# The causal stage's division of the probabilities by their row sum: from VectorE (three heads) and ScalarE (one) to GpSimd (all four)

## The reference, cut to what matters

```python
scores = einsum('bhqd,bhkd->bhqk', q, k) / sqrt(64)
scores = where(causal, scores, finfo.min)
attn = softmax(scores, axis=-1)      # exp(x - max), divided by the row's sum
out = einsum('bhqk,bhkd->bhqd', attn, v)
```

## Time and profile before

| what | us |
|---|---|
| time, median of 3 runs | 1265.08 (1264.76 to 1265.37) |
| the profiled execution: its time | 1265.95 |
| the profiled execution: its span | 1264.1 |
| causal stage, first to last score | about 516 to 958 |
| one round of the causal stage | 55.8 |

### The profile page before, as it was taken

How to read it: one execution, slowest core, us unless ns; L and a number is a source line. 1 busy time by engine, 2 the same in 40 slices (tenths; PEclk the granted TensorE clock), 3 DMA queues, 4 the chain that set the end, 5 groups by cost and what they waited for, 6 DMA issues and landing times.

```text
span 1264.1 us, 27532 instructions
## 1 busy us (share of the span) xinstructions
PE 1079.2 (85%) x7484; PEld 982.7 (78%) x7484; DVE 1011.4 (80%) x3184; ACT 777.1 (61%) x2299; POOL 327.9 (26%) x544
## 2 busy tenths in 40 slices
PE   4699999999999992899999999999997349989892
PEld 1478888878888882689999989999996338888892
DVE  5599998989899998688888888888886716665655
ACT  2266666666566663688787878777776315554541
POOL 4455554545545448000000101000000220000013
PEclk9599999999999997699999999999999559999997
DMA  8600000000000000000000000010000345554413
GB/s 308 205 23 2 23 22 1 21 1 21 8 15 21 1 1 22 22 1 23 2 21 0 21 0 21 5 66 0 1 1 12 105 151 149 148 158 138 134 44 102
DMA packets 37400, 63.78 MB, mean 50 GB/s; under 512 B 3419, under 2 KB 23707, under 8 KB 37147
## 3 DMA queue, kind: packets, MB, share of 16 engines
q1 hardware_dynamic: 28604, 51.69, 13.1%
q10 hardware_dynamic: 7168, 6.88, 1.7%
q0 software_dynamic: 1536, 4.20, 1.1%
HBM read 45.92 MB, written 16.84 MB: 50 GB/s over the span
## 4 chain that ended last, share of the span: by engine, by line
PE 64%; DVE 16%; issue 8%; ACT 6%; DMA 2%; POOL 1%; ACTq 1%; DVEq 1%; SPq 1%; POOLq 0%
PE psO L621 14%; PE psS L593 9%; PE psX L604 8%; PE psP L640 8%; PE psY L675 5%; PE psS L792 4%; PE psX L792 3%; PE psT L651 3%; DVE pbuf L1185 3%; PE psT L660 2%; PE psO L813 2%; PE psP L813 2%; DVE pbuf L1201 2%; DVE bufB L1207 2%; DVE bufA L1243 1%
## 5 line engine op out<-in xcount | busy, mean ns | idle before, releaser
L880 ACT ACTIVATE pbuf<-pbuf,nmax 128x256 f32<-128x256 f32 (+3 forms) x512 | 266.9, 522 | 172.9 <-DVE nmax L1185 162.3
L621 PE MATMUL psO<-bufB 128*128 128x256 f32 x1632 | 257.4, 294 | 11.9 <-DVE bufB L1211 11.2
L593 PE MATMUL psS<-bufA 128*128 128x256 f32 (+3 forms) x1024 | 216.5, 317 | 19.9 <-DVE bufA L1243 16.9
L621 PEld LDWEIGHTS psO<-bufB 128*128 128x128 f32 x1632 | 213.5, 190 | 23.1 <-issue 12.7
L1207 DVE TENSOR_TENSOR bufB<-psX,bufB 128x512 fp32r<-128x512 f32 x272 | 186.7, 686 | 29.0 <-ACT bufB L853 27.0
L853 ACT ACTIVATE bufB<-psX 128x512 fp32r<-128x512 f32 x272 | 160.4, 590 | 59.5 <-PE psO L621 48.8
L593 PEld LDWEIGHTS psS<-bufA 128*128 128x128 f32 x1024 | 149.4, 194 | 37.5 <-DVE nmax L1185 26.0
L604 PE MATMUL psX<-idn,pbuf 128*128 128x128 f32 x1088 | 167.2, 276 | 2.7 <-DVE bufB L1207 2.2
L640 PE MATMUL psP<-wbufs,hTh 128*128 (+1 forms) x512 | 163.0, 360 | 1.6 <-DVE bufB L1236 1.6
L1201 DVE TENSOR_SCALAR pbuf<-pbuf,rden 128x256 f32<-128x256 f32 (+3 forms) x384 | 154.3, 457 | 4.5
L604 PEld LDWEIGHTS psX<-idn,pbuf 128*128 128x128 f32 x1088 | 124.5, 141 | 18.0 <-issue 8.4
(11 more groups left out here) (196 smaller groups left out, 2304.0 us busy)
## 6 DMA issues: line engine op xcount, KB each, us to landing
mrawV<-in_w_moe SPq DMA_DIRECT2D x32, 384.0 KB, 3.2
mrawB<-in_w_moe SPq DMA_DIRECT2D x32, 384.0 KB, 3.3
xg<-uN SPq DMA_DIRECT2D x1, 5248.0 KB, 23.8
yg<-uN SPq DMA_DIRECT2D x1, 5248.0 KB, 37.9
xin<-xg ACTq DMA_DIRECT2D x10, 384.0 KB, 3.8
wraw<-in_w_attn SPq DMA_DIRECT2D x8, 384.0 KB, 3.2
wraw<-in_w_ffn SPq DMA_DIRECT2D x8, 384.0 KB, 3.0
yg<-modb ACTq DMA_DIRECT2D x9, 256.0 KB, 2.2
```

The lines of the kernel that those rows point to most:

```text
L593: last = mm(psS[j % 2][:, 0:n], qT[:, s % NT, j * P:(j + 1) * P], kT[:, c, k0:k0 + n], start=(c == 0), stop=(c == 1))
L621: last = mm(psO[:, 0:2 * P], lhsT, pairs(pT)[:, r], start=(k == 0 and n == 0), stop=(k == L.ntiles(s) - 1 and n == 5))
L880: nc.scalar.activation(pj, pj, ACT.Exp, bias=nmax[:, s % 4, j:j + 1], scale=-1.0, accum_out=sums[:, s % 4, j:j + 1]).then_inc(a_exp, 1)
```

## The change

In the causal stage GpSimd now multiplies all four heads by the reciprocal. It does so in its step s for the unit s-1, in front of that step's `split_piece`. VectorE keeps the reciprocal, VectorE and ScalarE lose their multiplications, and PE waits for one semaphore, `g_norm`, in place of two. The windowed stage stays as it was.

```diff
 def step(g, s, L=L):                      # GpSimd
     ...
+    if L is LB and exists(g, s - 1):
+        wait(pool, v_rden, L.unit(g, s - 1))
+        n = L.ntiles(s - 1) * P
+        for j in range(QM):
+            pj = probs[:, (s - 1) % 4, j, 0:n]
+            apart(pool)
+            last = nc.gpsimd.tensor_scalar(pj, pj, rden[:, (s - 1) % 4, j:j + 1], None, ALU.mult)
+        last.then_inc(g_norm, 1)
     if s in (0, 1, 2) and exists(g, NT):
         split_piece(g + 1, s)

 def turn_probs(g, s, k):                  # TensorE
-    if k == 0:
+    if k == 0 and L is LA:
         wait(pe, v_norm, L.unit(g, s))
         wait(pe, a_norm, L.unit(g, s))
+    elif k == 0:
+        wait(pe, g_norm, L.unit(g, s) - NT * NKV)

 def normalise(g, s):                      # ScalarE
     wait(act, v_rden, L.unit(g, s))
-    for j in range(L.by_vector, QM):
+    for j in range(L.by_vector, QM if L is LA else 0):
...
-    last.then_inc(a_norm, 1)
+    if L is LA:
+        last.then_inc(a_norm, 1)

 def normalise(g, s):                      # VectorE
...
+    if L is LB:
+        return
     for j in range(L.by_vector):
```

More of the change, by code:

```diff
@@ L334, in build @@
         a_norm = sem("a_norm")
+        g_norm = sem("g_norm")
         s_X = sem("s_X")
```

## The result

The changed kernel takes 1313.62 us in the median (1310.91 to 1315.83, 4 runs) against 1265.00 us before (1264.76 to 1265.37, 4 runs). The ratio is 1.0386 with an interval of 1.0362 to 1.0410: slower by 48.6 us. The forecast was 1312 us. The profiled execution took 1313.7 us with a span of 1311.9.

What follows compares the result with a forecast made beforehand. The prediction took TensorE, busy 96.5 of 100 us, to bound the causal stage. Its terms, 28.6 + 8.1 + 2.4 + 9.2 - 1.6 = +46.7 us on a median of 1265.08, gave 1312 us, range 1274 to 1345.

Steps and rivals of the forecast that it cites:

- Term 1: Rounds 1 to 6: tile 2's division queues behind a weight piece waiting for TensorE; six pauses of 4.8 us, +28.6 us.
- The price of a multiplication: On GpSimd, taken from its one-operation TENSOR_SCALAR: 1.53 us at length 512, 1.20 us at 384.
- rivals A and B: GpSimd multiplies at the CAST's price, 1276 us, chance 0.13; or nearer its two-operation price, about 1395 us, chance 0.1.
- Term 2: 512-long units elsewhere in the causal stage: GpSimd's division comes 0.9 us late for TensorE, nine times, +8.1 us.
- Term 3: End of the causal stage: GpSimd finishes the last division at 965.6, TensorE took these probabilities at 963.15, +2.4 us.
- Term 4: TensorE's clock falls behind four of the six long pauses, 2.3 us each: +9.2 us, bounds 0 and 13.8.
- The relief (-1.6): VectorE's saved multiplications shorten TensorE's 0.26 us pause for the key write by 0.1 us, 16 times: -1.6 us.
- The sum: 28.6 + 8.1 + 2.4 + 9.2 - 1.6 = +46.7 us, added to the median of 1265.08 us.

Runs made afterwards that it cites:

- three heads: Changed kernel with GpSimd dividing heads 0 to 2 and ScalarE head 3: ratio 1.0251; with the third weight piece also issued one step later, 0.9997.
- one instruction: Changed kernel with GpSimd dividing all four heads in one two-input multiplication, third weight piece left in step 2: 1291.54 us, ratio 1.0195.
- two heads: Changed kernel with GpSimd dividing heads 0 and 1 only, VectorE head 2, ScalarE head 3, third weight piece in step 2: 1289.86 us, ratio 1.0201.
- one head: Changed kernel with GpSimd dividing head 0 only, VectorE heads 1 and 2, ScalarE head 3, third weight piece in step 2: 1305.32 us, ratio 1.0273.
- single instruction: Changed kernel with one two-input multiplication for all four heads and the third weight piece issued in step 3: 1264.78 us, ratio 0.9972.
- piece 2 a step later: Changed kernel with GpSimd's third weight piece issued in step 3 instead of 2, behind the division of tile 2: 1283.93 us, ratio 1.0149.

## Why the prediction was right, point by point

**The blocked division (Term 1, +28.6).** Right and shown. Six pauses of 4.74 to 4.76 us, 28.5 in all, and one moved line removes them. The formula also holds over the dose. With the piece (2.10 us in the prediction, 2.05 in the expectations), the division, 0.15 for the wake-up and 2.13 off, it gives, forecast against measured: four heads 4.8 against 4.75; three heads 3.7 against 3.54; one instruction 2.8 against 2.57; two heads 2.5 against 2.32; one head 1.3 against 0.73. It is up to 0.25 us too long, and 0.6 us at one head, of which 0.35 is TensorE's own lateness there.

**The price of a multiplication.** 1.53 us forecast and 1.564 measured at 512, 1.20 and 1.242 at 384. The row to go by was the TENSOR_SCALAR of the same kind in the earlier trace rows, not the CAST, and rivals A and B fell with it. At 128 and 256 it is 605 and 924 ns, so the fixed part is nearer 0.29 than 0.2 us. The rule of the Trainium skill ("GPSIMD Engine Reference", section 4.1) that one-input work runs roughly at line rate does not hold for this instruction: the same 512 elements take 610 ns as a CAST and 1564 ns here.

**The 512-long units (Term 2, +8.1).** Nine pauses of 0.71 to 0.82 us, about 7.0 in all. That tile 3 of rounds 1 to 6 is forgiven was right: with the long pause gone, these six came back. With 5.4 us or less for the division the pause is gone altogether, as three heads and the single instruction showed.

**The stage's end (Term 3, +2.4).** The last pause is 2.52 us, and one of 1.32 us stands ahead of it. They took the place of pauses of 1.57 and 0.60 us for VectorE's `bufB`, so +1.7 net. Behind the last the clock fell for 3.4 us, about 3.4 x (1 - 1/1.8) = 1.5 us lost: 3.2 in all.

**The clock (Term 4, +9.2).** The term that was mis-sized, by its count. All six long pauses had a fall behind them, not four, and so had the last pause of the stage. Here are the stretches of the kernel before, of the changed one and of that with piece 2 a step later (columns as in the earlier trace rows):

```profile
529.23:977.24 448.01, 426.24 (x3207) 403.79 (x3207) 389.26 (x1286) 352.14 (x1046) 29.30 (x36) 1.00 0.03 11
524.16:1026.15 501.99, 443.66 (x3206) 418.42 (x3206) 343.90 (x1097) 327.28 (x983) 302.62 (x293) 0.96 0.04 11
526.67:990.47 463.80, 428.85 (x3207) 403.54 (x3207) 343.71 (x1097) 327.02 (x983) 302.67 (x293) 1.00 0.04 12
```

TensorE does the same matmuls in all three (one record is missing in the second). It is busy 17.4 us longer in the changed kernel, and 2.6 us longer with the piece moved, where it never works at half clock: some 0.15 us for each of 17 pauses. The other 14.8 us belong to seven falls, 2.1 us each, so the price of 2.3 us was near enough. I had taken from the earlier trace rows that a pause of 2.4 us leaves the clock at 1.00. The same pause of the windowed stage looks otherwise in the kernel without division:

```profile
477.75 0.98 PE L624 MATMUL psO<-bufB 128*128 128x256 f32 x6 [2.41 <-DVE bufB L1217]
```

```profile
480.00:482.00 2.00, 2.00 (x11) 2.00 (x11) 1.07 (x3) 0.98 (x2) 0.41 (x1) 0.50 0.02 4
```

With one head, and with one instruction not moved, it had a fall behind it too. In the causal stage pauses of 2.57 us had one six times in six and 2.32 us four times in six; of the two of 2.5 us at the stage's end (changed, and piece 2 later) one; those of 0.8 us none. So what follows a pause of 2.3 to 2.5 us differs with the same work around it, and one row of one execution was too little to build on.

**The relief (-1.6).** Measured -1.9 without any division. The size was right by luck. It was to come from the pauses of 0.26 us, which stayed as they were; it came from the first round and the stage's end. I had also named `add_y` as the start of the round trip; moving it left the pauses as they were, and the trip starts with the scores of head 2 behind it. The conclusion, that the pause of 0.62 us starts with TensorE and so can't be relieved, holds with that correction.

**The sum.** By the three rows, TensorE's idle time in the stretch grew from 21.8 to 58.3 us, +36.6, where pauses and relief were put at 28.6 + 8.1 + 2.4 - 1.6 = 37.5. Its busy time grew by 17.4, where the clock was put at 9.2. Against the median the forecast of +46.7 met +48.6, and that closeness is partly luck: a sum 7.3 us short against the stretch was offset by an earlier rise of the clock ahead of it, as far as the two profiled executions show.

**What stays open:** why equal pauses of 2.32 us had a fall behind them at four places and not at two, and whether fetched instructions are what stalled VectorE at the loop's start with one head.

## What to carry to other kernels

An engine that is 10% busy is not free at every moment: before giving it work with a due time, look at what stands ahead of that work in its queue and what that waits for, since here one weight copy that waited for TensorE turned a hidden division into six pauses of 4.8 us. A pause of the bounding engine can have a second price in its clock; here it was about 2.1 us behind four of six pauses of 2.32 us and behind all the longer ones in the middle of the stage. Work taken off an engine that is 89% busy is worth only the pauses that its work causes: here 62.7 us of VectorE's multiplications were worth 1.9 us.

## What was not expected of the hardware

**One two-input instruction is cheaper than four one-input ones.** On GpSimd a TENSOR_TENSOR with the column of scalars broadcast takes 3602, 2750 and 1897 ns for 2048, 1536 and 1024 elements, 1.67 ns for each element more; a TENSOR_SCALAR takes 1564 - 605 = 959 ns for 384 elements more, 2.5 ns each.

**GpSimd and VectorE slow each other while both divide.** GpSimd's 128x512 TENSOR_SCALAR, mean over the whole span:

```profile
L525 POOL TENSOR_SCALAR pbuf<-pbuf,rden 128x512 f32<-128x512 f32 x32 | 52.0, 1636 | 42.3 <-DVE rden L1210 42.3
```

```profile
L525 POOL TENSOR_SCALAR pbuf<-pbuf,rden 128x512 f32<-128x512 f32 x16 | 28.6, 1785 | 80.1 <-DVE rden L1210 80.1
```

The first is the kernel with two heads, the second that with one; with three or four heads, where VectorE divides nothing, it is 1566 and 1564 ns. VectorE's own division of that shape has a mean of 483 ns in the kernel before, 538 with two heads on GpSimd and 702 with one (530 to 950 us). The Trainium skill ("SBUF — State Buffer", Who interferes with whom) says that a `tensor_scalar` of VectorE can take, for its whole length, the pair of ports that it shares with GpSimd. The rows agree that the two hold each other up, with 0.07 and 0.22 us more on 1.56; that it is by the ports no run here shows.

**A loop start can stall an engine for 4.3 us** although its program differs by one instruction a unit (one head against two), as told above; its cause is open.
